# Attention scores in two row groups at once, the causal mask added in the maximum, a third query bank, and the maximum's rows sent by ScalarE's queue

## The reference, in short

```python
xn = x * rsqrt(mean(x * x) + EPS) * norm_w                # x here is already layer-normed
q, k, v = (xn @ W.T + b).reshape(B, T, 16, 8)             # 16 heads of 8 features
scores = einsum('bhqd,bhkd->bhqk', q, k) / sqrt(8)
scores = where(causal, -inf, scores)                      # key after query: masked
out = einsum('bhqk,bhkd->bhqd', softmax(scores), v) @ Wo.T + bo
x = x + xn + out
```

## Time and profile before

| what | value |
|---|---|
| median of 3 runs | 318.89 us |
| the profiled execution | 317.4 us, span 315.3 us |
| granted TensorE clock, mean | 0.961 |
| busy over the span: PE, DVE, ACT, POOL | 271.4, 212.2, 149.2, 185.7 us |
| key side of sequence 0 begins, of 1, of 5, of 7 | 123.58, 137.05, 192.29, 219.33 us |
| first token dispatch of the last mixture | 233.44 us |

### The profile page before, as it was taken

The page is one execution under the profiler, slowest core; times in us unless marked ns, Lnnn a source line. Parts: engine busy times, 40 slices in busy tenths (PEclk is TensorE's granted clock), DMA queues, the critical chain, the costliest instruction groups (busy, mean ns, idle before and its releaser), DMA issues.

```text
span 315.3 us, 7921 instructions
## 1 busy us (share of the span) xinstructions
PE 271.4 (86%) x2368; PEld 219.5 (70%) x2368; DVE 212.2 (67%) x685; ACT 149.2 (47%) x362; POOL 185.7 (59%) x332
## 2 busy tenths in 40 slices
PE   7724999999997778999989999998977759999980
PEld 6724999999994544656656565665646658999970
DVE  4956058888539568986657777776587744888860
ACT  2300076666206613676656667666541007666620
POOL 7587815445726313786767787888647740555561
PEclk9999999999999996999999999999976799999997
DMA  6974232221041733552433522110001143122100
GB/s 184 397 313 122 60 80 55 68 67 32 17 133 41 202 109 112 165 166 87 135 95 115 157 74 70 58 55 2 5 10 45 56 113 91 49 68 67 30 21 0
DMA packets 34388, 29.37 MB, mean 93 GB/s; under 512 B 4109, under 2 KB 28818, under 8 KB 34353
## 3 DMA queue, kind: packets, MB, share of 16 engines
q1 hardware_dynamic: 29696, 23.52, 25.1%
q0 software_dynamic: 2496, 4.27, 4.3%
q10 hardware_dynamic: 2160, 1.14, 1.4%
HBM read 17.08 MB, written 12.55 MB: 94 GB/s over the span
## 4 chain that ended last, share of the span: by engine, by line
PE 48%; POOL 16%; issue 9%; DMA 9%; DVE 9%; SPq 4%; ACT 2%; POOLq 1%; ACTq 0%; DVEq 0%
PE bank L1291 12%; PE bank L1302 11%; POOL disp_d L479 7%; PE bank L1448 4%; PE bank L1420 3%; PE bank L1396 3%; POOL pT L574 2%; PE bank L1426 2%; DMA row<-in_x 2%; PE bank L1393 2%; SPq L406 2%; POOL row L470 2%; PE bank L1283 2%; PE bank L1401 2%; DMA disp_d<-row,slot 2%
## 5 line engine op out<-in xcount | busy, mean ns | idle before, releaser
L746 ACT ACTIVATE pT<-bank 128x512 f32<-128x512 f32 x96 | 56.5, 600 | 43.0 <-PE bank L1426 29.2
L1056 DVE TENSOR_REDUCE mh<-bank 128x2 f32<-128x512 f32 x64 | 42.1, 683 | 10.1 <-PE bank L1396 9.9
L1302 PE MATMUL bank<-experts,hT 128*128 x368 | 48.9, 276 | 0.0
L1291 PE MATMUL bank<-xsT,ew 128*128 128x128 f32 x368 | 48.8, 276 | 0.1
L1222 PE MATMUL bank<-zero 128*128 128x128 f32 x268 | 37.3, 305 | 10.5 <-DVE rowi L934 4.7
L574 POOL TENSOR_SCALAR_AFFINE_SELECT pT<-pT 128x512 f32<-128x512 f32 x62 | 40.2, 651 | 9.4 <-ACT pT L746 9.3
L1302 PEld LDWEIGHTS bank<-experts,hT 128*128 128x128 f32 x368 | 44.8, 192 | 0.5 <-issue 0.3
L1291 PEld LDWEIGHTS bank<-xsT,ew 128*128 128x128 f32 x368 | 44.7, 192 | 0.5 <-issue 0.2
L1222 PEld LDWEIGHTS bank<-zero 128*128 128x128 f32 x268 | 35.8, 219 | 11.0 <-DVE rowi L934 4.7
L664 ACT ACTIVATE hT<-bank,ew 128x128 f32<-128x128 f32 x92 | 28.9, 365 | 28.7 <-PE bank L1291 28.7
L941 DVE TENSOR_SCALAR hT<-bank,ew 128x128 f32<-128x128 f32 x92 | 28.0, 346 | 21.3 <-PE bank L1291 19.9
(11 more groups left out here) (140 smaller groups left out, 465.9 us busy)
## 6 DMA issues: line engine op xcount, KB each, us to landing
sp_d<-spl SPq DMA_DIRECT2D x32, 192.0 KB, 2.5
experts<-in_experts SPq DMA_DIRECT2D x8, 578.0 KB, 9.5
qz<-sp_d SPq DMA_DIRECT2D x32, 96.0 KB
ks<-sp_d SPq DMA_DIRECT2D x32, 96.0 KB
xs_sb<-disp_d SPq DMA_DIRECT2D x46, 66.0 KB, 1.9
row<-in_x SPq DMA_DIRECT2D x4, 256.0 KB, 5.2
row<-x_d SPq DMA_DIRECT2D x4, 256.0 KB, 3.6
disp_d<-pad ACTq DMA_DIRECT2D x12, 66.0 KB
```

Of the source, the lines that this page charges most:

```text
L746: act.activation(pT[:, u, :], bank[2 + u % 2][:, :], ACT.Exp, scale=SCALE).then_inc(a_e, 1)
L1056: dve.tensor_reduce(mh[:, half, 1, :, 2 * pp + w], bank[u % 2][:, :].rearrange("p (h n) -> p h n", h=2), AX.X, ALU.max).then_inc(a_mx, 1)
L1291: mm = pe.matmul(bank[2 + 2 * (k % 2) + c // 2][:, (c % 2) * P:(c % 2 + 1) * P], ew[:, k % WRING, c * P:(c + 1) * P], xsT[:, k % 2, :], st ...
L1302: mm = pe.matmul(bank[6 + k % 2][:, 0:D], hT[:, k % 2, c, :], w2.rearrange("p a c -> p (a c)"), start=(c == 0), stop=(c == HC - 1))
```

## The change

- `ks` and `qz` hold head j = 0 in rows 0 to 47 and head j = 1 in rows 64 to 111 (`JBASE`), each with its own three maximum rows behind it. The other head's zeros are no longer needed, so the zero fill is gone.
- A unit holds heads of one j only: units 0, 1, 4, 5 are two heads of 256 columns, units 2 and 3 four heads of 128. In a round the key side takes j = u % 2 and the query side the other j, and PE issues them alternately, product by product.
- The mask product is left out for sequences 1 to 7; DVE's `tensor_tensor_reduce` adds a mask table to each head's scores, writes them back to the bank and returns the maximum, one instruction per head. Sequence 0 keeps the mask product and one reduction per unit.
- Query-side units go round banks 0, 1 and 6. Turned maxima, both turned outputs, turned normalised outputs and the projection share bank 7.
- The maximum's rows are sent by ACT in two transfers, right after its copy of them, in place of one by SP.
- Values of the first pair move from u = 4 to u = 5, projection and its addition to the next sequence's first unit, and one turn of outputs to the second half's first unit. The projection of sequence 6 comes after the loop; on DVE its addition stays between the two last masks, which now are unit 3's and that of units 4 and 5.
- The loops are written out, and with them four small instructions per half on POOL (`turn`, L569) go.

```diff
+JBASE = P // 2
+KROWS = JROWS + 3
+QB = (0, 1, 6)
...
-                sp.wait_ge(a_mtc, 2 * b + half + 1)
-                sp.dma_start(qz[k][MROW:MROW + 3, half, :, :, :].rearrange("s j i n -> s (j i n)"), mT[:, half, :]
-                             ).then_inc(a_m[half], 16)
...
-                pool.memset(qz[k][:, :, :, :, :].rearrange("p h j i n -> p (h j i n)").bitcast(F32), 0.0
-                            ).then_inc(static_s, 1)
-                    pool.tensor_tensor(turn[:, n:n + 1], zero[:, 0:1], zero[:, 0:1], ALU.add)
+                pool.wait_ge(a_e, 12 * b + 6 * half + (2, 3, 4, 6)[n])
...
-                need(act, a_pv, 2 * (2 * b + half - 1) + 1 + u // 3
-                     if not isinstance(b, int) or 2 * b + half > 0 else 0)
+                need(act, a_pv, 2 * (2 * b + half - 1) + (1 if u < 2 else 2)
+                     if 2 * b + half > 0 else 0)
...
+                act.copy(mT[:, half, :], bank[7][0:24, 0:P].bitcast(BF16)).then_inc(a_mtc, 1)
+                act.wait_ge(a_mtc, 2 * b + half + 1)
+                for j in range(2):
+                    act.dma_start(qz[b % 2][JBASE * j + JROWS:JBASE * j + KROWS, half, :, :].rearrange(
+                        "s i n -> s (i n)"), mT[12 * j:12 * j + 12, half, :]).then_inc(a_m[half], 16)
...
+                late, p0, heads = unit(u)
+                top = mh[:, half, 0 if late else 1, 1 - u % 2, p0:p0 + heads]
+                if b == 0:
+                    i1 = dve.tensor_reduce(top, bank[QB[u % 3]][:, :].rearrange("p (h n) -> p h n", h=heads),
+                                           AX.X, ALU.max)
+                else:
+                    n = 512 // heads
+                    for m in range(heads):
+                        sc = bank[QB[u % 3]][:, m * n:(m + 1) * n]
+                        i1 = dve.tensor_tensor_reduce(sc, sc, msk[:, T - n:T], 1.0, LOWEST, ALU.add, ALU.max,
+                                                      top[:, m:m + 1])
...
+                if u == 0:
+                    pe.wait_ge(a_m[half], 32 * (b + 1))
+                need(pe, a_e, 12 * b + 6 * half + u - 1)
+                if more:
+                    scores_q_waits(b + 1, half, u)
+                for m in range(unit(u)[2]):
+                    mk = scores_k_part(k, half, u, m)
+                    if more:
+                        mq = scores_q_part(b + 1, half, u, m)
...
+                    if (half, u) == (0, 0) and b >= 2:
+                        project(b - 2)
+                    if (half, u) == (0, 2):
+                        pe.wait_ge(a_mtc, 2 * b + 1)
+                        need(pe, a_x, b - 1)
+                        turn_max(b, 1)
+                    if (half, u) == (0, 4) and not first:
+                        pe.wait_ge(a_mtc, 2 * b + 2)
+                        turn_out(b - 1, 0)
+                    if u == 5:
                         pv(b, k, half, 0)
+                    if (half, u) == (1, 0) and not first:
+                        pe.wait_ge(a_an, 2 * b - 1)
+                        turn_out(b - 1, 1)
+                    if (half, u) == (1, 4) and not first:
+                        if more:
+                            pe.wait_ge(a_mtc, 2 * b + 3)
+                        turn_norm(b - 1)
```

More of the change, by code:

```diff
@@ L322, in scattered, with unit @@
             return 16 * (f * len(range(k, NS, OUT)) + n)
+        def unit(u):
+            late = u in (2, 3)
+            return late, 0 if late else 2 * (u // 4), 4 if late else 2
         def units(n):
@@ L598, in _ @@
                 step(0, half)
-            with pool.Fori(0, 2) as i:
-                for k in range(2):
-                    for half in range(2):
-                        step(2 * i + 1 + k, half)
-            for b in (5, 6, 7):
+            for b in range(1, B):
                 for half in range(2):
@@ L771, in step @@
                         out_copy(b if half else b - 1, 1 - half)
-                    if u == 3 and half == 1 and not first:
+                    if u == 4 and half == 1 and not first:
                         act.wait_ge(a_aT, b)
@@ L786, in _ @@
             step(0, 1, True, first=True)
-            with act.Fori(0, 2) as i:
-                for k in range(2):
-                    for half in range(2):
-                        step(2 * i + 1 + k, half, True)
-            for b in (5, 6, 7):
+            for b in range(1, B):
                 for half in range(2):
@@ L1152, in _ @@
                 step(0, 0, half, True, first=True)
-            with dve.Fori(0, 2) as i:
-                for k in range(2):
-                    for half in range(2):
-                        step(2 * i + 1 + k, 1 - k, half, True)
-            for b in (5, 6):
+            for b in range(1, 7):
                 for half in range(2):
                     step(b, b % 2, half, True)
+            add_out(5)
             def late_stats(q):
@@ new lines, in scores_q_waits, with scores_q_part @@
+                    pe.wait_ge(a_stk[b % 2][half], 64 * (b // 2 + 1))
+                need(pe, a_mx, 12 * b + 6 * half + u - 2)
+            def scores_q_part(b, half, u, m, masked=False):
+                late, p0, heads = unit(u)
+                n = 512 // heads
+                q_, k_ = head(b % 2, half, p0 + m, 1 - u % 2, JROWS)
+                return pe.matmul(bank[QB[u % 3]][:, m * n:(m + 1) * n], q_[:, 0:P] if late else q_[:, P:T], k_[:, 0:n],
+                                 start=not masked, stop=True, **(MM_BANK if masked else {}))
@@ new lines, in scores_k_part, with scores_first @@
+            def scores_k_part(k, half, u, m):
+                late, p0, heads = unit(u)
+                n = 512 // heads
+                q_, k_ = head(k, half, p0 + m, u % 2, KROWS)
+                return pe.matmul(bank[2 + u % 2][:, m * n:(m + 1) * n], k_[:, P:T] if late else k_[:, 0:P],
+                                 q_[:, T - n:T], start=True, stop=True)
+            def scores_first(half, u):
+                scores_q_waits(0, half, u)
+                heads = unit(u)[2]
+                pe.matmul(bank[QB[u % 3]][:, :].rearrange("p (h n) -> p h n", h=heads)[:, :, 512 // heads - P:],
+                          ident_b, maskS.unsqueeze(1).broadcast_to((P, heads, P)), start=True, stop=False, **MM_BANK)
+                for m in range(heads):
+                    mm = scores_q_part(0, half, u, m, masked=True)
@@ L1480, in project, with step @@
                 mm.then_inc(a_wo, 1)
-            def step(b, bh, k, half, more, first=False):
+            def step(b, half, more, first=False):
+                k = b % 2
                 for u in range(6):
-                    scores_k(b, k, half, u)
-                    if more:
-                        scores_q(b + 1, bh, 1 - k, half, u)
+                    scores(b, k, half, u, more)
                     if u == 1 and half:
```

226 lines of the change are left out of this document (79 added, 147 removed).

## The result

The changed kernel takes 368.32 us (median of 4 runs, 364.67 to 370.56) against 318.77 (317.56 to 320.3) for the kernel before: a ratio of 1.151, 95% interval 1.141 to 1.162. The profiled run, the slowest of the four at over 1.5% above the fastest, is left out of the ratio. The changed kernel is 50 us slower; the prediction was 311, with a range up to 329. The profiled execution took 370.6 us, its span is 368.8, and its mean granted clock 0.822 (before: 0.961).

What follows compares the result with a forecast made beforehand. PE was taken to set the pace; from 317.4 us, sequences 1 to 4 gave −6.1, 5 and 6 −1.8, sequence 0 +0.5, the end +0.3: 310.3, stated as 311 for the median, range 304 to 329 for 8 in 10.

Steps and rivals of the forecast that it cites:

- the ring: Chain through ScalarE from a half's last maximum to the next half's last: 6.5 us, then 5.5 without output copy and turn.
- its own signs of being wrong: Fused maxima over 0.43 and 0.30 apart, clock below 1 from 127 to 215 us, or half A 6.7 while DVE idles.
- half A: Sequence's step for heads of half 0, with values, normalise and projection's addition on DVE: ring 6.5 us, DVE 6.0.
- side by side: Key-side and query-side products sharing PE's array: 0.22 us per unit, PE 4.5 per half; in turn 5.8, chance 0.07.
- e: What each fused maximum on DVE pays to hand its result out: 0.045 us, the middle of 0.02 and 0.07.
- the dear maximum: Slower rival on DVE: fused maxima's result hand-outs at 0.14 us each make 328 us; chance 0.18.
- half B: Sequence's other step, its ring without output copy and turn: ring 5.5 us, DVE 5.5.
- the issues: ACT issuing the maximum's rows in two transfers after its copy: 1.1 to 1.56 us, taken as 1.1.
- The clock: Slower rival: PE's 2.5 us wait in half A halves its clock once per sequence, +14.4, 325 us; chance 0.14.
- Stall: PE's 1.69 us wait for the maximum's rows behind SP's loads and stores: taken as gone, at worst +1.7.
- The end: Sequence 6's projection behind the last half's first values, its addition on DVE before the last mask: +0.3 us (0 to 1).
- First scores: Start of the attention stage: one more bank against 0.6 of work moved ahead, put at 0.

Runs made afterwards that it cites:

- e6: Changed kernel with dummy matmuls in both of TensorE's waits of a sequence, 9 in half A and 7 in half B: 344.7 us.
- e7: Changed kernel with the maximum's rows sent by SP's queue and 4 dummy matmuls at each of the two waits: 331.0 us, ratio 1.037.
- e4: Kernel before with one part alone: the maximum's rows sent by ScalarE's queue, one transfer per half: 325.7 us, ratio 1.024.
- e1: Changed kernel with 16 dummy matmuls once per sequence, in TensorE's wait for the copied attention output: 368.9 us.
- e14: Changed kernel with rows by SP's queue and both products of a unit in one row group, one after the other: 379.5 us.
- e2: Changed kernel with both products of a unit from the same row group, so they can't run side by side: 393.7 us, ratio 1.239.
- e10: e7 with bank 6 instead of shared bank 7 for the second output turn, from sequence 6's output on: 326.6 us, ratio 1.024.
- e9: Changed kernel with rows by SP's queue, and the mask product on TensorE with a plain maximum on VectorE: 341.2 us, ratio 1.063.
- e12: Kernel before with VectorE adding the mask in a fused maximum from the second sequence on, no TensorE mask product there: 318.99 us, ratio 1.003.

## Why the prediction was wrong

The prediction summed a full-speed TensorE and a ring of 6.5 and 5.5 us. Both failed, the ring first; no rival of its list came near 368 (the dearest was 328). Two of its own signs of being wrong came: the clock is below 1 between 127 and 215 us, and half A takes 9.7 to 11.0 us in sequences 1 to 4 of the changed kernel while VectorE idles.

**PE.** Right in kind: side by side, and PE no longer the bound. A unit is 0.33, not 0.22, where an instruction over all 128 rows comes next, since that starts 0.1 after the products' end; another unit follows at 0.23 (e6, 185.03 to 185.26). Five of six units are of the first kind, so the six are 1.9 instead of 1.32. By e7's window PE is busy 41.62/7 = 5.9 per half, less 0.9 of dummies 5.0 (forecast 4.5).

**DVE.** Right: 0.38 and 0.25 between fused maxima, where 0.385 and 0.255 were forecast (e was the middle of its bounds, so that it fits to 0.005 is luck), and in e7 busy 6.3 and 5.6 in halves A and B, where 6.0 and 5.5 were. The Trainium skill (VectorE: DVE Perf Modes, "Two Vector instructions with no wait between them") is borne out: each fused maximum has its accumulator read as a second instruction, 0.13 long. It lies over the next one, so it adds 0.04 to the pitch of an addition and no more; the dear maximum was not the rival that came.

**The ring: the step that failed first.** It was put at 6.5 in half A and 5.5 in half B, a sequence at 12.3. At full clock (e6) the halves take 7.8 and 7.3 from sequence 4 on, when the clock has held for three, 15.1 a sequence. Two terms: the issues, 1.1 by the lower end of the bounds, take 1.5 (SP's 0.78 was the nearer row); and the way back from the next exponential to the next split. The prediction led it over PE's unit and DVE's last maxima: 0.60 + 0.58 + 0.45 + 0.22 + 0.77 = 2.6 in half A and 0.60 + 0.22 + 0.77 = 1.6 in half B, without hops. It leads over the last exponential and POOL's mask of it, behind which the split stands in POOL's order: 194.53 to 198.63, 4.1 us, and 187.41 to 190.42, 3.0 us. That order was there to be read in the kernel before, in front of the split of the earlier trace rows:

```profile
166.20 0.64 POOL L574 TENSOR_SCALAR_AFFINE_SELECT pT<-pT 128x512 f32<-128x512 f32 x1
```

e4 shows the size without any clock: 0.9 us a sequence for one issue per half, +7.7 us in all.

**The clock: a rival, with one of two waits and a price too small.** It was to fall once a sequence, for the 2.5 us wait in half A, and to cost 2.4 there, 14.4 in all. That wait is there (2.64), and the clock falls at its end; so it does at the end of half B's wait of 1.70, which the prediction did not have. e1 filled the first and left the second, and the fall moved to the second; e6 filled both, and the clock held until PE stood idle from 246 to 248. Not every wait is followed by a fall (155.6 to 159.1), and waits do not explain all: e14 has none over 0.7 and stays low. The Trainium skill (TensorE: Matmul & The Clock Gate, Part 1) says that how busy the engine has been sets the gate. The alternation at 188 to 200 looks like it; e14's 57.77 busy of 60 us at 0.50 disagrees, and the measurement decides. What is shown: 1.6 to 2.1 us of full-array dummies in each half bring 1.00 back for 102 us (e6), and a sequence falls from 18.8 to 15.7 in sequences 1 to 4 and to 15.1 later, so 3.1 to 3.7 of the 5.0 lost per sequence are the clock and the rest is the ring. The two costs feed each other: rows by SP gain 32.8 us without dummies (368.3 to 335.5), 13.7 with them (344.7 to 331.0, with fewer of them in the second). What brings the clock back up, or keeps it down in e2 and e14, stays open.

**Stall.** Gone, as forecast: PE waits nowhere for the rows in the changed loop. On SP the wait is back (e7, 6.2 us).

**No gain underneath.** With the issues moved and the clock held (e7) a sequence takes 13.5 to 13.9, forecast 12.3. It is not VectorE: in half B (6.15) PE with its dummies is busy 5.8, and half A adds the late rows. A kernel with full clock, without dummies and with the rows on time was not run, so what the change would gain there is not shown.

**The end.** Put at +0.3; it is 9.2 + 3.3. Bank 7's four users were followed through the ring only; in sequence 7 PE waits 2.6 us at it in the changed kernel (2.86 in e7) for VectorE, which is at the routing. e10 measures this part at 4.4; the rest goes with a clock of 0.50 from 268 to 282 and 285 to 302 us. **First scores.** Put at 0, +4.9 here with the clock at 0.50 from 114.5 to 124.8; kernels with the same or nearly the same code up to there began between 0.3 (e14) and 6.5 us (e9) late. Why was not tried, nor were the written-out loops of PE, ACT and POOL; those of VectorE alone cost nothing (e12).

## What to carry to other kernels

An engine that has stopped being the bound can still set the pace: ask what clock it will be granted, and take a forecast of "half as busy" as a risk, not as slack. Write a ring down as the engines' own instruction order has it, each queued instruction between the two ends, before pricing its steps; a transfer's issue is work of the engine that issues it. And measure parts alone: here the rows' move lost 2.4% by itself, the mask's move nothing, the layout with side-by-side products 6.3% (e9), and the sum 15%.

## What the runs showed of the hardware

- TensorE was granted 2.4 GHz and 1.2 GHz at the same busy share (0.96: the kernel before and e14).
- TensorE's clock fell to 1.2 GHz at the end of waits of 2.64 and 1.70 us (changed kernel, sequence 3) and just behind one of 1.79 us (e1), and held at 2.4 GHz for 102 us when both waits of a sequence were filled (e6).
- A transfer of three short rows costs ScalarE mostly 0.73 to 0.75 us of issue (e4 and the changed kernel; two took 1.79 once in e6), and the next instruction starts another 0.1 later (changed kernel).
- Products in two row groups start 10 ns apart, into different banks, and the array takes 0.1 us more before its next full-height instruction (0.33 after the unit's start, against 0.23 before another such unit).
